# Small attention heads: each head's keys alone in a zero-padded 128-row tile, with a new state-space order and activation

## The chip, the cores and the metric

The kernel runs on one core of a Trainium2 chip. The metric is device microseconds of one launch. The time before is the median of three runs.

## The reference

Two layers of a hybrid network on an input of 4 x 512 tokens with 256 features, in float32. Each sublayer adds its output to x after a layer norm:

```python
x = x + state_space(ln(x))      # in-projection, conv of 4, silu, scan, gate, out-projection
x = x + ffn0(ln(x))
x = x + rotary_attention(ln(x)) # 16 heads of 16
x = x + ffn0(ln(x))
x = x + latent_and_pattern(ln(x))  # latent attention and 16 plain heads of 16, mixed by a gate
x = x + ffn1(ln(x))
x = x + grouped(ln(x))          # 32 query heads of 8 over 8 key heads, and a memory term
x = x + ffn1(ln(x))
```

The state-space recurrence is `h = exp(delta * A) * h + delta * B * u`, `y = C * h`, along 512 steps. Attention is `softmax(q @ k.T * scale) @ v` per head. The memory term of the grouped sublayer is

```python
sigma_q = jax.nn.elu(q.reshape(b, s, N_QUERY, D_KV))
a_mem = sigma_q @ memory / (sigma_q @ memory_norm)
out = a_dot * (1.0 - w) + a_mem * w      # w = sigmoid(memory_weight)
```

## The kernel before, in words

x stays in the core's memory, 128 features by 2 by 2048 tokens, and four batches of 512 tokens are worked on in turn. Nine stages follow each other (`PLAN`): state space, ffn0, rotary, ffn0, pattern, latent, ffn1, grouped, ffn1. A stage starts when the one before has ended on all engines (`stage_start`, line 183). Constants and weights come by SP's DMA queue; POOL cuts weights into a high and a low part (`cut_pieces`, line 209), and three matmuls of such parts (`mm3`, lines 226 to 228) stand for one product. The order on each engine is a list of events written out by hand; every engine walks the same list and does its share of each event, in that order, waiting on counters of the others.

**State space** (`mamba`, line 334; events at 364 to 394). In a batch: `wx` (in-projection on PE, copied by ACT), `conv` (four DVE operations, lines 592 and 596), `u` (silu on ACT, line 528), `u cut` (high part on ACT, line 534, low on POOL, line 438), `wz`, `steps` (a narrow product for delta, line 480), `one` and `delta` (softplus on ACT and DVE), then for each of four feature tiles `B` and `C` (12 matmuls each), `step` (spreads delta, line 500; ACT makes `a bar` from it, line 557) and `scan` (six DVE operations, lines 620 to 637, the first `du`, the last the gated product), `y cut` (line 564), and `out` in the next batch. The front of a batch (`mean`, `squared`, `var`, `dev`, `xn`, `xn cut`) is the layer norm; `dev` is a root on ACT (line 305).

**Small heads** (`Heads`, line 932) serve three stages: rotary and pattern with two heads to a 128-row tile (64 rows each, `per` = 2) and grouped with four (32 rows each). Four heads make a group g; there are 16 groups in rotary and in pattern and 32 in grouped. Selection matmuls (lines 1069 and 1070) stack queries (`eq`) and keys (`ek`) of a group from the high and low parts; ACT copies the stacks to `QS` and `KS` (lines 1101 and 1105), the keys with a row of ones. In rotary and pattern a group has two key tiles, in grouped the keys are stacked once a batch, two tiles. Then `mx`: 16 matmuls per group (line 1074), each followed by a maximum over keys on DVE (line 1137). `bias` (line 1079) turns the maxima, and DVE adds them to a row of the query stack (line 1143). `s` makes the scores, keys as weights (line 1084), ACT takes the exponential (line 1116), `pv` multiplies with the values, four heads side by side in 32 columns each (line 1091). Scores have three PSUM banks, other products four in turn.

A unit is a group and one of four key tiles `kt`. `schedule` (line 983) emits the four `s` of a unit with one to four `mx` of the next group between them, then the `pv` of the unit before, then what is in the slot: stacks two groups ahead after the last unit of a group, norms, projections of the next batch, and so on, set by `heads.put`.

```python
nc.tensor.matmul(self.psum(ev), self.QS[r, g % 2, h // self.per, q * P:(q + 1) * P],
                 self.k_of(g, self.k_tile_no(g, h))[r, :], start=True, stop=True)
```

Here `r` is the head's 64 or 32 rows, so a matmul uses those rows of the array alone.

**Grouped** (line 2155) adds the memory term: `qk`, then `tanh` (lines 2273 and 2278), `elu` (three DVE operations, lines 2330 to 2334, a reciprocal among them), `elu sum` on POOL (2300), `memory norm` and `memory` (fp32 products, line 2245), added to the attention by DVE (2351, 2354). For the first batch both halves of it stand in the start of the stage.

Of the kernel before, what the change touches and what calls it, by code (L numbers as in the profile page):

```python
# [18 lines left out]
F32 = mybir.dt.float32  # L19
F32R = mybir.dt.float32r  # L20
# [5 lines left out]
P = 128  # L26
# [123 lines left out]
def build(nc, io, out, plan, table):  # L150
    ctx = ExitStack()
    with ctx:
# [3 lines left out]
        def sem(name):  # L156
            return ctx.enter_context(nc.semaphore(name))
# [22 lines left out]
        x_in, c_in, stored = sem("x_in"), sem("c_in"), sem("stored")  # L180
# [153 lines left out]
        def mamba():  # L334
# [111 lines left out]
            def pe(pe, s):  # L446
# [7 lines left out]
                for ev in events:  # L454
# [6 lines left out]
                    if kind in ("mean", "var"):  # L461
                        if kind == "var":
                            pe.wait_ge(A.sem, A.at((s, ("squared", b))))
# [102 lines left out]
            def vec(dve, s):  # L566
# [13 lines left out]
                for ev in events:  # L580
                    kind, b = ev[:2]
                    if kind in ("mean", "var", "xn"):
                        if kind == "mean" and b:
                            dve.wait_ge(G.sem, G.at((s, ("xn cut", b - 1))))
# [347 lines left out]
        class Heads:  # L932
# [4 lines left out]
            def __init__(self, alloc, heads, width, rows, khead, scale, q_tile, k_tile, k_tiles, c, C, SEL):  # L937
# [10 lines left out]
                self.KS = alloc("k_stack", [P, 2, k_tiles or self.tiles, L], F32R)  # L948
# [27 lines left out]
            def k_of(self, g, t):  # L976

                return self.KS[:, (g // self.G4) % 2, t % self.k_tiles, :] if self.k_tiles else self.KS[:, g % 2, t, :]
# [1725 lines left out]
```

## Time and profile before

| | us |
|---|---|
| median of three runs | 4672.29 (4657.89 to 4677.12) |
| the profiled execution | 4669.16 |
| its span | 4667.3 |
| PE busy / DVE / ACT / POOL | 3906.4 / 2615.7 / 1657.6 / 1294.5 |
| state space, from start to 313 | 313 |
| ffn0, twice | 236 and 234 |
| rotary, 549 to 1063 | 514 |
| pattern, 1297 to 1746 | 449 |
| latent, 1746 to 2759 | 1013 |
| ffn1, twice | 560 and 560 |
| grouped, 3319 to 4101 | 782 |

The stages are read from the DMA that loads each stage's constants. PE is the busiest engine; matmuls overlap in the pipeline, and a busy share of PE is no share of its peak. The granted TensorE clock is given as a share of 2.4 GHz and is a mean over 0.5 and 1.0. Its mean over the span is 0.871.

### The profile page before, as it was taken

What the parts mean: (1) busy time and instruction counts of PE and PEld (TensorE: products, weight loads), DVE (VectorE), ACT (ScalarE), POOL (GpSimd) and SP (SyncE); (2) the same over time, 40 slices, a digit from 0 to 9 for tenths busy, and PEclk for the clock granted to TensorE, in tenths of its full rate; (3) what the DMA queues carried; (4) which work ended last, traced back from release to release, by engine and by line L of the source; (5) the groups of instructions that cost most, each with busy time, mean ns of one, the idle gap of its engine ahead of it and who ended that gap; (6) DMA issues with size and microseconds to landing.
All of it is one profiled execution on the core that took longest, in us unless ns stands there. A gap on an engine that the chain in (4) does not pass through costs nothing.

```text
span 4667.3 us, 44375 instructions
## 1 busy us (share of the span) xinstructions
PE 3906.4 (84%) x15840; PEld 2512.2 (54%) x15840; DVE 2615.7 (56%) x4363; ACT 1657.6 (36%) x2773; POOL 1294.5 (28%) x1034
## 2 busy tenths in 40 slices
PE   5769778887978874889889868999688888879999
PEld 4547544435844432556556647888433333347887
DVE  5545356654456643777777756333366666645333
ACT  2323246653235540333333323222244444422222
POOL 3224322214321003232323224443201110143442
PEclk8879889988979976999999989999866676679999
DMA  1010000001000001000000010000000000010000
GB/s 55 0 37 4 29 1 1 1 1 40 1 21 5 5 20 68 25 19 25 19 23 19 25 49 24 24 20 1 15 1 1 1 1 1 0 53 21 28 12 19
DMA packets 31815, 83.27 MB, mean 18 GB/s; under 512 B 6256, under 2 KB 7408, under 8 KB 31216
## 3 DMA queue, kind: packets, MB, share of 16 engines
q1 hardware_dynamic: 31600, 80.44, 5.5%
q8 instruction: 130, 2.13, 0.2%
q14 instruction: 85, 0.70, 0.1%
HBM read 59.44 MB, written 4.19 MB: 14 GB/s over the span
## 4 chain that ended last, share of the span: by engine, by line
PE 55%; DVE 21%; ACT 4%; POOL 2%; issue 2%; DMA 1%; SPq 1%; DVEq 0%; POOLq 0%; ACTq 0%
PE ps L226 10%; PE ps L227 10%; PE ps L228 10%; DVE max_cols L1137 6%; PE ps L1091 6%; PE ps L1084 3%; PE ps L1923 2%; PE ps L296 2%; DVE max_cols L2116 2%; DVE q_lo L2100 2%; PE ps L1074 2%; PE ps L1079 1%; ACT probs L1116 1%; PE ps L801 1%; PE ps L1069 1%
## 5 line engine op out<-in xcount | busy, mean ns | idle before, releaser
L1137 DVE TENSOR_REDUCE max_cols<-ps 128x1 fp32r<-128x512 f32 x1024 | 634.5, 680 | 274.2 <-PE ps L1074 249.1
L1116 ACT ACTIVATE probs<-ps 128x512 f32<-128x512 f32 x1024 | 538.3, 604 | 297.8 <-PE ps L1074 216.0
L755 POOL TENSOR_TENSOR h_lo<-h,h_hi 128x512 fp32r<-128x512 f32 x304 | 391.8, 1289 | 820.8 <-ACT h_hi L835 820.8
L912 DVE TENSOR_TENSOR gated<-silu,ps 128x512 f32<-128x512 f32 x288 | 198.0, 687 | 692.8 <-PE ps L228 664.5
L829 ACT ACTIVATE silu<-ps 128x512 f32<-128x512 f32 x304 | 181.7, 598 | 933.5 <-PE ps L228 933.3
L226 PE MATMUL ps<-xn_hi,w_hi 128*128 128x512 f32 x1216 | 481.5, 396 | 0.0
L227 PE MATMUL ps<-xn_lo,w_hi 128*128 128x512 f32 x1216 | 477.5, 393 | 0.0
L228 PE MATMUL ps<-xn_hi,w_lo 128*128 128x512 f32 x1216 | 477.0, 392 | 0.0
L1084 PE MATMUL ps<-q_stack,k_stack 64*128 64x512 f32 (+1 forms) x1024 | 415.6, 544 | 68.2 <-ACT probs L1116 63.9
L1074 PE MATMUL ps<-k_stack,q_stack 64*128 64x512 f32 (+1 forms) x1024 | 362.6, 532 | 80.1 <-DVE max_cols L1137 17.4
L1091 PE MATMUL ps<-probs,v_aug 128*32 128x512 f32 x2048 | 364.9, 794 | 0.0
L1084 PEld LDWEIGHTS ps<-q_stack,k_stack 64*128 64x128 f32 (+1 forms) x1024 | 171.2, 219 | 339.4 <-ACT probs L1116 175.7
L330 POOL CAST o_hi<-o_scaled 128x512 fp32r<-128x512 f32 x64 | 39.0, 610 | 1042.6 <-DVE o_scaled L1159 1042.6
L1923 PE MATMUL ps<-probs,v_tok 128*128 128x512 f32 x512 | 262.4, 609 | 2.7 <-ACT denominators L1985 2.7
L226 PEld LDWEIGHTS ps<-xn_hi,w_hi 128*128 128x128 f32 x1216 | 232.1, 191 | 50.0 <-issue 1.0
L227 PEld LDWEIGHTS ps<-xn_lo,w_hi 128*128 128x128 f32 x1216 | 231.5, 190 | 49.9 <-issue 1.5
L228 PEld LDWEIGHTS ps<-xn_hi,w_lo 128*128 128x128 f32 x1216 | 231.0, 190 | 48.9
L226 PE MATMUL ps<-h_hi,w_hi 128*128 128x512 f32 x608 | 250.2, 411 | 1.2 <-POOL h_lo L755 1.2
L1074 PEld LDWEIGHTS ps<-k_stack,q_stack 64*128 64x128 f32 (+1 forms) x1024 | 159.6, 216 | 165.7 <-ACT probs L1116 94.2
L227 PE MATMUL ps<-h_lo,w_hi 128*128 128x512 f32 x608 | 240.6, 396 | 0.0
L228 PE MATMUL ps<-h_hi,w_lo 128*128 128x512 f32 x608 | 240.4, 395 | 0.0
L1975 ACT ACTIVATE probs<-ps 128x1024 f32<-128x1024 f32 x128 | 131.1, 1024 | 279.3 <-PE ps L1920 279.2
(453 smaller groups left out, 7563.0 us busy)
## 6 DMA issues: line engine op xcount, KB each, us to landing
raw<-in_w_ffn SPq DMA_DIRECT2D x76, 448.0 KB, 3.3
raw<-raw SPq DMA_DIRECT2D x256, 64.0 KB, 2.0
composed_inputs<-in_m_latent SPq DMA_DIRECT2D x1, 5120.0 KB, 15.5
raw<-in_w_mamba SPq DMA_DIRECT2D x8, 448.0 KB, 6.1
raw<-in_w_latent SPq DMA_DIRECT2D x5, 448.0 KB, 16.8
x<-in_x SPq DMA_DIRECT2D x1, 2048.0 KB, 7.8
gated_pattern<-gated SPq DMA_DIRECT2D x4, 512.0 KB, 3.4
raw<-gated_pattern SPq DMA_DIRECT2D x4, 512.0 KB, 4.2
```

Of the source, the lines that this page charges most:

```text
L226: nc.tensor.matmul(psum, wh, xh, start=start, stop=False)
L227: nc.tensor.matmul(psum, wh, xl, start=False, stop=False)
L228: return nc.tensor.matmul(psum, wl, xh, start=False, stop=stop)
L755: nc.gpsimd.tensor_tensor(HL[:, b % 3, :], hb[:, b % 2, :], HH[:, b % 3, :].bitcast(F32), ALU.subtract).then_inc(G.sem, G.step((s, ev)))
L829: nc.scalar.activation(sg[:, i % 2, :], bank[i % 2], ACT.Silu).then_inc(A.sem, A.step((s, ev)))
L912: nc.vector.tensor_tensor(ga if routed(i) else hb[:, i % 2, :], sg[:, i % 2, :], bank[2 + i % 2], ALU.mult).then_inc(V.sem, V.step((s, "ga ...
L1074: last = nc.tensor.matmul(self.psum(ev), self.QS[r, g % 2, h // self.per, q * P:(q + 1) * P], self.k_of(g, self.k_tile_no(g, h))[r, :], st ...
L1084: last = nc.tensor.matmul(self.scores(self.step_no(g, kt, h)), self.k_of(g, self.k_tile_no(g, h))[r, kt * P:(kt + 1) * P], self.QS[r, g % ...
L1091: last = nc.tensor.matmul(bank[6][32 * h:32 * h + 32, :], self.VA[:, (g // self.G4) % 2, kt, self.khead((g % self.G4) * 4 + h), :], self.P ...
L1116: nc.scalar.activation(self.PB[:, n % 8, :], self.scores(n), ACT.Exp, scale=self.scale).then_inc(A.sem, A.step((s, ("exp", n))))
L1137: nc.vector.tensor_reduce(self.MB[:, self.tile_of(g, h) % 2, q, col:col + 1], self.psum(ev), op=ALU.max, axis=AX.X, negate=True).then_inc( ...
L1923: last = nc.tensor.matmul(bank[6 + i], VT[:, (g // HP) % 2, kt, 64 - 64 * i:192 - 64 * i], PB[:, (g * QT + kt) % 2, i, :], start=kt == 0, ...
```

## The change

Keys of each head stand alone in a 128-row tile whose other rows are zero (`KZ`, zeroed once by DVE at the start of a stage), so `mx` and `s` take all 128 rows of the query stack; the other heads' query rows meet zeros. ACT writes a key stack head by head: two operations in rotary and pattern, four in grouped, for one. In the state-space stage the event list is reordered and x is loaded in four DMAs. In grouped the elu becomes relu(q) + tanh(n/2) * (exp(n) + 1), with n = min(q, 0), its sums on POOL and no reciprocal; the first batch's memory term moves into the loop; the memory term is added to x by POOL.

```diff
             events = [(kind, 0) for kind in front] + [("wx", 0, m) for m in every] + [("conv", 0, m) for m in every]
-            events += [(kind, 1) for kind in front[:4]]
+            events += [(kind, 1) for kind in front[:4]] + [("u", 0, m) for m in every]
             for b in range(NB):
                 near, far = b + 1 < NB, b + 2 < NB
-                events += [("u", b, m) for m in every] + [("u cut", b, m) for m in every] + [("wz", b, m) for m in every]
+                events += [("u cut", b, m) for m in every] + [("wz", b, m) for m in every]
...
                 events += [("B", b, 0), ("one", b)]
-                events += [("wx", b + 1, 0), ("conv", b + 1, 0)] if near else []
+                events += [("wx", b + 1, 0)] if near else []
                 events += [("C", b, 0), ("delta", b)]
-                events += [("wx", b + 1, 1)] if near else []
-                events.append(("B", b, 1))
-                events += [("wx", b + 1, 2)] if near else []
-                events.append(("C", b, 1))
-                events += [("wx", b + 1, 3)] if near else []
-                events += [("step", b, 0), ("step", b, 1)]
-                events += [("conv", b + 1, 1)] if near else []
-                events += [("scan", b, 0), ("y cut", b, 0)]
+                events += [("wx", b + 1, 1), ("conv", b + 1, 0)] if near else []
+                events += [("step", b, 0), ("B", b, 1), ("step", b, 1), ("scan", b, 0), ("y cut", b, 0), ("C", b, 1)]
+                events += [("wx", b + 1, 2), ("conv", b + 1, 1), ("wx", b + 1, 3)] if near else []
+                events += [("scan", b, 1), ("y cut", b, 1)]
                 events += [("mean", b + 2), ("squared", b + 2)] if far else []
                 events += [("B", b, 2), ("step", b, 2), ("C", b, 2)]
-                events += [("conv", b + 1, 2)] if near else []
-                events += [("scan", b, 1), ("y cut", b, 1)]
-                events += [("var", b + 2)] if far else []
-                events += [("B", b, 3), ("step", b, 3), ("C", b, 3), ("scan", b, 2), ("y cut", b, 2)]
-                events += [("conv", b + 1, 3)] if near else []
+                events += [("conv", b + 1, 2), ("conv", b + 1, 3)] if near else []
+                events += [("scan", b, 2), ("y cut", b, 2)]
+                events += [("var", b + 2), ("dev", b + 2)] if far else []
+                events += [("B", b, 3), ("step", b, 3), ("C", b, 3)]
+                events += [("u", b + 1, m) for m in every] if near else []
                 events += [("scan", b, 3), ("y cut", b, 3)]
-                events += [("dev", b + 2)] if far else []
...
-                self.KS = alloc("k_stack", [P, 2, k_tiles or self.tiles, L], F32R)
+                self.alone = self.nkv if k_tiles else 4
+                self.KZ = alloc("k_alone", [P, 2, self.alone, L], F32R)
...
-                    r = slice((h % self.per) * self.rows, (h % self.per + 1) * self.rows)
-                    last = nc.tensor.matmul(self.psum(ev), self.QS[r, g % 2, h // self.per, q * P:(q + 1) * P],
-                                            self.k_of(g, self.k_tile_no(g, h))[r, :], start=True, stop=True)
+                    last = nc.tensor.matmul(self.psum(ev), self.q_rows(g, h)[:, q * P:(q + 1) * P], self.k_rows(g, h),
+                                            start=True, stop=True)
...
+                    if g == 0:
+                        act.wait_ge(V.sem, V.at((s, "alone")))
+                    for i in range(self.per):
+                        r = slice(i * self.rows, (i + 1) * self.rows)
+                        to = self.KZ[r, (g // self.G4 if self.k_tiles else g) % 2, t * self.per + i, :]
+                        nc.scalar.activation(to, self.psum(ev)[r, :], ACT.Identity, bias=self.one[r, :]).then_inc(A.sem, A.step((s, ev)))
...
+                nc.vector.memset(self.KZ[:, :, :, :].bitcast(F32), 0.0).then_inc(V.sem, V.step((s, "alone")))
...
+            a0, a1 = memory(0, 0), memory(0, 1)
+            heads.put(0, 0, 8, *a0[1])
+            heads.put(0, 1, 5, *a0[2])
+            heads.put(0, 0, 4, a1[0][0])
+            heads.put(0, 1, 8, a1[0][1])
+            heads.put(0, 2, 3, *a1[1])
+            heads.put(0, 2, 9, *a1[2])
+            begin = [(kind, 0) for kind in front] + [("qk", 0, 2)] + a0[0] + [("v", 0, q) for q in range(QT)]
...
-                        nc.scalar.activation(el, negative, ACT.Tanh, scale=0.5).then_inc(A.sem, A.step((s, ev)))
+                        act.wait_ge(G.sem, G.at((s, ("tanh",) + ev[1:])))
+                        nc.scalar.activation(half_tanh, negative, ACT.Tanh, scale=0.5).then_inc(A.sem, A.step())
+                        nc.scalar.activation(power, negative, ACT.Exp).then_inc(A.sem, A.step())
+                        nc.scalar.activation(whole, whole, ACT.Relu).then_inc(A.sem, A.step((s, ev)))
...
+                        nc.gpsimd.tensor_tensor(whole, CH[:, m, :].bitcast(F32), CL[:, m, :].bitcast(F32), ALU.add).then_inc(G.sem, G.step())
+                        pool.wait_ge(G.sem, G.last())
+                        nc.gpsimd.tensor_scalar(negative, whole, 0.0, None, ALU.min).then_inc(G.sem, G.step((s, ev)))
...
+                        nc.gpsimd.tensor_scalar(power, power, 1.0, None, ALU.add).then_inc(G.sem, G.step())
+                        pool.wait_ge(G.sem, G.last())
+                        nc.gpsimd.tensor_tensor(half_tanh, half_tanh, power, ALU.mult).then_inc(G.sem, G.step())
...
+                        nc.gpsimd.tensor_tensor(el, whole, half_tanh, ALU.add).then_inc(G.sem, G.step((s, ev)))
...
-                        nc.vector.tensor_scalar(t0, el, -1.0, 1.0, ALU.mult, ALU.add).then_inc(V.sem, V.step())
-                        after_last()
-                        nc.vector.reciprocal(t0, t0).then_inc(V.sem, V.step())
-                        after_last()
-                        nc.vector.scalar_tensor_tensor(t0, el, 2.0, t0, ALU.mult, ALU.mult).then_inc(V.sem, V.step((s, ev)))
...
-            sp.dma_start(x[:, :, :], io["x"]).then_inc(x_in, 16)
+            for b in range(NB):
+                sp.dma_start(x[:, :, b * L:(b + 1) * L], io["x"][:, :, b * L:(b + 1) * L]).then_inc(x_in[b], 16)
```

## Rows read from the trace of the kernel before

**Rows 1.** Windows: PE, PEld, DVE, ACT, POOL busy (count), clock, DMA share, GB/s.
```profile
640.00:1063.00 423.00, 359.26 (x1594) 173.80 (x1592) 266.13 (x444) 250.22 (x441) 87.86 (x80) 0.90 0.00 1
...
1352.00:1746.00 394.00, 328.93 (x1538) 164.14 (x1538) 233.94 (x392) 199.39 (x371) 40.35 (x38) 0.88 0.02 6
...
3395.00:4101.00 706.00, 597.80 (x2466) 234.11 (x2464) 459.55 (x749) 332.77 (x626) 77.93 (x76) 0.68 0.00 1
```
**Rows 2.** Windows of 20 us, in grouped and in rotary, same columns.
```profile
3480.00:3500.00 20.00, 17.83 (x76) 8.19 (x72) 11.23 (x20) 8.03 (x17) 0.43 (x1) 0.57 0.00 1
...
680.00:700.00 20.00, 18.43 (x83) 8.75 (x83) 12.94 (x22) 11.70 (x22) 1.90 (x2) 1.00 0.00 1
```
**Rows 3.** Timeline of PE: start, us, operation; two like units of grouped.
```profile
3495.80 1.94 PE L1091 MATMUL ps<-probs,v_aug 128*32 128x512 f32 x8
...
3501.29 1.08 PE L1091 MATMUL ps<-probs,v_aug 128*32 128x512 f32 x4
...
3676.37 1.06 PE L1091 MATMUL ps<-probs,v_aug 128*32 128x512 f32 x8
...
3679.76 0.64 PE L1091 MATMUL ps<-probs,v_aug 128*32 128x512 f32 x4
```
**Rows 4.** Timeline of PE: first of eight score and maximum matmuls, and what follows.
```profile
3418.64 0.79 PE L1084 MATMUL ps<-q_stack,k_stack 32*128 32x512 f32 x2
...
3421.26 1.94 PE L1091 MATMUL ps<-probs,v_aug 128*32 128x512 f32 x8
```
**Rows 5.** Timeline of PE at full clock, grouped.
```profile
3597.05 0.40 PE L2258 MATMUL ps<-o_lo,h_grouped_hi 128*128 128x512 f32 x1
3597.38 0.50 PE L1084 MATMUL ps<-q_stack,k_stack 32*128 32x512 f32 x1
3597.38 0.50 PE L1074 MATMUL ps<-k_stack,q_stack 32*128 32x512 f32 x3
...
3598.57 0.50 PE L1084 MATMUL ps<-q_stack,k_stack 32*128 32x512 f32 x1 [0.27 <-ACT probs L1116]
```
**Rows 6.** Timeline of the state-space stage, all engines, about its second batch.
```profile
119.38 0.63 ACT L564 ACTIVATE y_hi<-y 128x512 fp32r<-128x512 f32 x1 [8.15 <-DVE y L637]
...
122.95 2.19 ACT L528 ACTIVATE u<-u 128x512 f32<-128x512 f32 x4
...
127.75 0.63 PE L226 MATMUL ps<-u_hi,rate_hi 128*32 128x512 f32 x1 [9.88 <-ACT z L540]
...
142.96 2.33 DVE L596 SCALAR_TENSOR_TENSOR u<-padded,c,u 128x512 f32<-128x512 f32 x3
...
156.81 0.69 DVE L620 TENSOR_TENSOR du<-u,ps 128x512 f32<-128x512 f32 x1 [6.04 <-PE ps L296]
```
**Rows 7.** Timeline of pattern: stacks on ACT, then PE's fourth score matmul.
```profile
1447.85 0.69 ACT L1101 ACTIVATE k_stack<-ps,c 128x512 fp32r<-128x512 f32 x1 [2.33 <-PE ps L1070]
...
1448.43 0.59 ACT L1105 ACTIVATE q_stack<-ps 128x512 fp32r<-128x512 f32 x1
...
1450.62 0.49 PE L1084 MATMUL ps<-q_stack,k_stack 64*128 64x512 f32 x1 [0.51 <-ACT probs L1116]
```
**Rows 8.** Chain that ended last, in the start of grouped: start, us, what.
```profile
3347.39 0.43 PE ps L228
...
3353.66 3.36 DVE t L2332
...
3357.82 1.27 POOL elu L2300
...
3363.34 0.23 PE ps L227
...
3377.20 0.11 PE ps L2252
```
**Rows 9.** Timeline of the start of grouped, DVE.
```profile
3322.50 1.76 DVE L1127 MEMSET v_aug<- 128x2048 f32 x1 [0.38 <-issue]
...
3332.54 1.28 DVE L313 TENSOR_TENSOR xc<-x,ps 128x512 f32<-128x512 f32 x2 [7.63 <-PE ps L296]
```

More of the change, by code:

```diff
@@ L179, in build @@
         gated_pattern = nc.dram_tensor("gated_pattern", (P, KD, T), F32, kind="Internal").ap()
-        x_in, c_in, stored = sem("x_in"), sem("c_in"), sem("stored")
+        x_in, c_in, stored = [sem(f"x_in{b}") for b in range(NB)], sem("c_in"), sem("stored")
         raws, c_loads = [0], [0]
@@ L461, in pe @@
                     if kind in ("mean", "var"):
-                        if kind == "var":
+                        if kind == "mean":
+                            pe.wait_ge(x_in[b], 16)
+                        else:
                             pe.wait_ge(A.sem, A.at((s, ("squared", b))))
@@ L582, in vec @@
                     if kind in ("mean", "var", "xn"):
-                        if kind == "mean" and b:
-                            dve.wait_ge(G.sem, G.at((s, ("xn cut", b - 1))))
+                        if kind == "mean":
+                            dve.wait_ge(x_in[b], 16)
+                            if b:
+                                dve.wait_ge(G.sem, G.at((s, ("xn cut", b - 1))))
                         front_vec(dve, s, ev, psum(ev) if kind != "xn" else None, xc, sq, dev, roots)
@@ L974, in maxima, with k_rows, q_rows @@
                 return [("mx", g, t * self.per + i, q) for t in range(self.tiles) for q in range(QT) for i in range(self.per)]
-            def k_of(self, g, t):
-                return self.KS[:, (g // self.G4) % 2, t % self.k_tiles, :] if self.k_tiles else self.KS[:, g % 2, t, :]
+            def k_rows(self, g, h):
+                if self.k_tiles:
+                    return self.KZ[:, (g // self.G4) % 2, self.khead((g % self.G4) * 4 + h), :]
+                return self.KZ[:, g % 2, h, :]
+            def q_rows(self, g, h):
+                return self.QS[:, g % 2, h // self.per, :]
             def k_tile_no(self, g, h):
@@ L1082, in pe @@
                     g, kt, h = ev[1:]
-                    r = slice((h % self.per) * self.rows, (h % self.per + 1) * self.rows)
-                    last = nc.tensor.matmul(self.scores(self.step_no(g, kt, h)),
-                                            self.k_of(g, self.k_tile_no(g, h))[r, kt * P:(kt + 1) * P],
-                                            self.QS[r, g % 2, h // self.per, :], start=True, stop=True)
+                    last = nc.tensor.matmul(self.scores(self.step_no(g, kt, h)), self.k_rows(g, h)[:, kt * P:(kt + 1) * P],
+                                            self.q_rows(g, h), start=True, stop=True)
                 elif kind == "pv":
@@ L1100, in act @@
                     act.wait_ge(PE.sem, PE.at((s, ev)))
-                    nc.scalar.activation(self.k_of(g, t), self.psum(ev), ACT.Identity, bias=self.one).then_inc(A.sem, A.step((s, ev)))
+                    if g == 0:
[4 more added lines that the diff above has]
+                        nc.scalar.activation(to, self.psum(ev)[r, :], ACT.Identity, bias=self.one[r, :]).then_inc(A.sem, A.step((s, ev)))
                 elif kind == "eq":
@@ L2184, in memory @@
             def memory(b, m):
-                return [[("qk", b, m), ("tanh", b, m)], [("elu", b, m), ("elu sum", b, m)], [("memory norm", b, m), ("memory", b, m)]]
+                return [[("qk", b, m), ("tanh", b, m)], [("elu", b, m)],
+                        [("memory norm", b, m), ("memory", b, m), ("memory added", b, m)]]
             for b in range(1, NB):
@@ L2190, in grouped @@
                 heads.put(b - 1, 1, 2, ("qk", b, 2))
[L2191 removed]
+                for m, j in ((0, 3), (1, 6)):
                     a = memory(b, m)
@@ L2201, in grouped @@
                     heads.put(b + 1, 0, 8, ("out", b, 1))
-            begin = [(kind, 0) for kind in front] + [("qk", 0, 2)] + sum(memory(0, 0), []) + sum(memory(0, 1), [])
-            begin += [("v", 0, q) for q in range(QT)]
+            a0, a1 = memory(0, 0), memory(0, 1)
[6 more added lines that the diff above has]
+            begin = [(kind, 0) for kind in front] + [("qk", 0, 2)] + a0[0] + [("v", 0, q) for q in range(QT)]
             heads.schedule(begin, [("out", NB - 1, 1)],
```

48 lines of the change are left out of this document (21 added, 27 removed).

## Prediction

> **What bounds the kernel now.** I read the window view by stage first, because the change touches four of nine stages. In the three small-head stages, once their start is over, the granted TensorE clock is 0.90 (rotary, 423 us), 0.88 (pattern, 394 us) and only 0.68 (grouped, 706 us), with PE busy 83% to 85% of each [rows 1]. The reader is to see that the low clock does not come with an idle PE: in two 20 us windows PE is busy 17.83 and 18.43 us, yet the clock is 0.57 in the one and 1.00 in the other [rows 2]. The first is in grouped, whose score matmuls have 32 rows, the second in rotary, where they have 64. In the chain, a series of 128-row matmuls begins at 0.43 us apiece (1.2 GHz) and is at 0.23 later (2.4 GHz) [rows 8]. So I take rows of the array, not busy time, as what the clock follows here. What the clock is worth stands in the timeline of PE: the same unit of work (one `pv` to the next) takes 5.49 us at clock 0.5 and 3.39 us at 1.0, so 38% of the slow time is lost [rows 3]. PE sets the end in both: its neighbours wait for it. In the state-space stage the bound alternates between PE and DVE: after the last gated product of a batch PE waits for ACT and POOL (to 127.75), and then DVE waits for PE and ACT (to 156.81) [rows 6].
>
> The sum is made against the profiled execution's 4669.2 us (span 4667.3 and 1.9 around it). The median of the runs is 3.1 us above, which I add at the end.
>
> **State-space order.** Before `step 0` PE no longer issues `B 1`, `wx 2`, `C 1`, `wx 3`: 36 matmuls of 0.23 us [rows 8], 8.3 us in batches 0 to 2, and 24, or 5.5 us, in batch 3 (no next batch): -30.4. Two things come back. One more convolution (2.33 us for three of its four operations [rows 6], 2.9 in all) stands inside DVE's scan chain where it stood ahead of it: +8.7. And the root `dev` now stands on ACT ahead of the last `a bar`. DVE's last scan waits for that, with nothing else in its queue, over two table loads, the root and the exponential. The 2.94 us between the end of `y hi` and the first `u` (loads and root) [rows 6] plus 0.6 make 3.5 us, in two batches: +7. At the border of batches, root, loads (2.9) and the four `u` activations (2.19) no longer stand between `y hi` and the step matmuls: -5.1 twice, and -3.5 once where there is no root: -13.7. Part sum **-28** (bounds -44 with nothing given back, 0 if DVE's chain takes it all). Four x loads for one: SP issues three more DMAs ahead of the constants, while the first mean needs a quarter of x: 0, bounds +2 and -2.
>
> **Rotary and pattern.** Each key stack becomes two ACT operations. Back to back they start 0.58 us apart [rows 7], two more per group. Queued behind them are the query stacks and the exponentials; the fourth score matmul of the next unit waits for the first of these already (0.51 us [rows 7]), and the `pv` and maxima for it. Nothing covers it, so 28 groups x 1.16 = **+33** (bounds 0 if later waits absorb it, +36 with those at the start).
>
> The score and maximum matmuls no longer run side by side. Four now share one stretch of 0.50 us [rows 5], and eight at 1.2 GHz take 2.62 us [rows 4] where eight 128-row ones of 0.43 would take 3.44: 0.8 more, 0.4 at full clock. Five of the eight stand before the fourth score matmul, which waits 1.19 us from the first for the exponentials anyway [rows 5]; five times 0.23 is 1.15, covered. The three behind it pay: 0.15 x 128 units = +19. Against that, every second border between unlike shapes costs about 0.1 us less (the step from a 128-row matmul at 3597.05 to the first score matmul is 0.33 [rows 5], against 0.23 between like ones): -8. Together **+11**.
>
> A rule speaks against the change here. First the row: a burst of eight that takes 2.62 us today cannot lose more than the 0.82 that single file adds [rows 4, 8], so side-by-side running saves a quarter and no more. The Trainium skill, "TensorE: Matmul & The Clock Gate", section "Part 3: Packing small matmuls", says to slice small contractions into distinct row groups, and gives 3.07x for four 32-row matmuls. By that ratio each of the 256 units would lose 1.2 us and the sum would be +171 instead of -123. The row excludes it, so it gets no chance of its own.
>
> Clock: (1 - 0.90) x 2 x 423 and (1 - 0.88) x 2 x 394 make 180 us at half clock [rows 1]. I take 60% of it as gone and 30% of that time as gained (less than the 38%, since more units here wait for ACT): **-32** (bounds 0 and -54).
>
> **Grouped.** 0.64 x 706 = 452 us at half clock [rows 1]. Between the 38% [rows 3] and some 28% where the unit waits for maxima I take 34%. If the stage ends at a clock of 0.92 (a little above rotary's, now that all score matmuls fill the array), about 93 us stay slow, so 359 x 0.34 = **-122** (bounds 0 and -154). Side-by-side lost: 19 less 6 = **+13**. Keys: eight ACT operations for two, 6 x 0.58 x 4 batches = **+14**. Activation: the two serial passes of the start (reciprocal 3.36 us on DVE, POOL, two fp32 products each) run from 3353.66 to 3377.20, 23.5 us [rows 8]. They leave it; their matmuls, about 9 us, return inside the loop, and some 2.5 us of the new POOL and ACT chain stay uncovered: **-12**. In the loop ACT is held for two POOL operations (1.27 each at most by [rows 8]) and two more of its own, about 2.3 us longer, six times (+14), while DVE loses 4.5 us of in-order work each time in front of maxima and bias. Half on the path is -14: **0**, bounds +20 and -20. New memory additions run on POOL, idle there most of the time. The large memset of the key tile is at most 4 x 1.76 = 7.0 us on DVE in grouped; it is hidden by the 7.63 us for which DVE waits for PE [rows 9], and would cost what sticks out, under 2 us. Sum **-107**.
>
> Total: -28 + 33 + 11 - 32 - 107 = **-123**, so 4546, and 4549 us beside the median.
>
> **Rivals.**
> *A, slower: the clock does not follow rows.* Then the grants stay, and the unpacked matmuls are paid at 1.2 GHz. In grouped 0.64 of 128 units pay 0.8 and the rest 0.15: +73, less 6, plus 14, less 12 = +69. Rotary and pattern +44, state space -28: +85, **4757 us**. For it: PE is already busy 85% and the grant still falls, and zeros add no work. Against it: [rows 2] and the rise within one 128-row series. With f the share of grouped's slow time that turns fast, and the other stages in step, the sum is about 85 - 240 f; it decides at f = 0.35, a clock in grouped of about 0.79. The skill's page "TensorE: Matmul & The Clock Gate", "Part 1", describes the grant as set by how busy the PE has been; taken as busy time alone, that rule gives this rival. Chance 0.09.
> *B: DVE and ACT become the bound in grouped.* DVE is busy 460 us of 706 [rows 1], some 420 after the reciprocals leave; PE at full speed needs 128 x (8 x 0.23 + 1.06) = 371 for scores, maxima and `pv` [rows 3, 8] and, an estimate, 120 for the rest. With both near each other, each maximum and bias waits in turn, and half of the clock's gain stays off: +61, **4610 us**. For: `bias` and `s` wait in turns on DVE and ACT already. Against: the 3.39 us unit contains those waits. Chance 0.22.
> *C: everything at full clock and the key copies absorbed.* -32 more in grouped, -22 in the other two, and up to -47 of key copies: **4448 us**. Chance 0.14.
> The forecast has 0.55.
>
> **How the numbers follow.** The range 4470 to 4645 holds the forecast with the bounds of the state-space term and of the key copies, B, and half of C. About 0.1 lies above (A and a little of B) and 0.08 below. A measurement of this kernel can tell about 0.5%, 23 us, from no change. Faster: forecast, C and nearly all of B, 0.87. Within 0.5%: 0.04, from B with the state-space gain lost. Slower: A, 0.09.
>
> **What would show it.** Right: grouped's granted clock at 0.88 or more and its stage near 675 us (782 now); score and maximum matmuls 128 rows deep, starting 0.23 us apart and not together; rotary and pattern within 15 us of before, with a longer wait for ACT in front of the fourth score matmul after each stack; state space near 285 us (313 now), its first `du` of a batch about 8 us nearer to the step matmuls. Wrong: a clock in grouped under 0.79; or a full clock with grouped above 720 us, DVE then busy over 80%; or rotary and pattern longer by more than 20 us each, which would put the key copies above what I priced.

## The result, and the profile after

The changed kernel takes 4604.62 us (median of 4 runs, 4602.95 to 4616.60) against 4674.70 for the kernel before on the same chip: ratio 0.986, 95% interval 0.983 to 0.989. By medians the gain is 70 us of the 123 forecast. The profiled execution took 4616.6 us, 12 above its median, with a span of 4614.8, so the two profiled spans are 52.5 us apart (70 short of the forecast), and the stages below add up to that. The mean granted clock rose from 0.871 to 0.919. Further down, every ratio is to runs of the kernel before on the same chip; its median was 4662 to 4675 us on the chips used.

First the stages, read as before from the DMA of each stage's constants on SP's timeline of the changed kernel.

```profile
294.39 0.33 SPq L728 DMA_DIRECT2D c<-in_c_ffn  x1
...
529.84 0.33 SPq L272 DMA_DIRECT2D c<-in_c_rotary  x1
...
1064.88 0.33 SPq L728 DMA_DIRECT2D c<-in_c_ffn  x1
...
1300.57 0.33 SPq L272 DMA_DIRECT2D c<-in_c_pattern  x1
...
1762.32 0.33 SPq L1755 DMA_DIRECT2D c<-in_c_latent  x1
...
2781.86 0.33 SPq L728 DMA_DIRECT2D c<-in_c_ffn  x1
...
3341.18 0.33 SPq L272 DMA_DIRECT2D c<-in_c_grouped  x1
...
4048.98 0.33 SPq L728 DMA_DIRECT2D c<-in_c_ffn  x1
```

| stage | before | after | change | forecast |
|---|---|---|---|---|
| state space | 313.1 | 294.4 | -18.7 | -28 |
| rotary and pattern | 514.2 + 449.3 | 535.0 + 461.8 | +33.3 | +12 |
| grouped | 782.2 | 707.8 | -74.4 | -107 |
| the five others | 2601.6 | 2609.1 | +7.5 | 0 |

The other five run the same code in both kernels; their sum ends where the output's DMA is issued, and the 7 us behind that are in both. Over all kernels here ffn0 came out between 230.5 and 236 us and latent between 1012 and 1023, so a difference of some 6 us in one stage of one profile is not read as an effect. The 461.8 of pattern is such a case: five other profiles below with the same code in that stage (e2, e3, e4, e7, e8) have 456.2 to 457.2, e7 at a clock of 0.97 where this one has 0.94. Rotary and pattern together are 988.1 to 994.7 us in those five (963.5 before, 996.8 here).

The windows that answer [rows 1], same columns: rotary, pattern, the start of grouped (64 us, 76 before), its loop.

```profile
622.00:1065.00 443.00, 376.48 (x1590) 201.29 (x1588) 266.75 (x444) 274.64 (x469) 87.94 (x80) 0.92 0.00 1
1357.00:1762.00 405.00, 337.35 (x1538) 189.90 (x1537) 234.15 (x392) 224.74 (x401) 40.54 (x38) 0.94 0.02 6
3341.00:3405.00 64.00, 32.60 (x88) 19.14 (x89) 29.20 (x39) 17.99 (x30) 15.67 (x15) 0.71 0.08 27
3405.00:4049.00 644.00, 539.14 (x2466) 277.10 (x2464) 428.38 (x722) 354.60 (x649) 128.50 (x113) 0.93 0.00 1
```

In grouped the clock went from 0.68 to 0.93 at an unchanged busy share of PE (85%, now 84%). ACT's busy time grew in all three, by 24 us in rotary: these are the key copies (in grouped the new activation's operations are among them).

The matmuls, PE's timeline in grouped, answer to [rows 5]. They now stand 128 rows deep and start 0.22 to 0.23 us apart, where four of 32 rows shared one stretch.

```profile
3693.73 0.39 PE L1079 MATMUL ps<-k_alone,q_stack 128*128 128x512 f32 x1
3693.96 0.39 PE L1088 MATMUL ps<-q_stack,k_alone 128*128 128x512 f32 x1
3694.18 0.62 PE L1079 MATMUL ps<-k_alone,q_stack 128*128 128x512 f32 x2
3694.64 0.39 PE L1088 MATMUL ps<-q_stack,k_alone 128*128 128x512 f32 x1
```

The stacks in pattern answer to [rows 7]. From the first copy to the first exponential ACT works without a pause for 3.95 us. In the kernel before, four such operations take 2 x 0.57 + 2 x 0.48 = 2.10 us. The fourth score matmul waits 1.56 us for ACT (0.51 before).

```profile
1382.80 1.39 ACT L1109 ACTIVATE k_alone<-ps,c 64x512 fp32r<-64x512 f32 x2 [1.48 <-PE ps L1076]
...
1384.21 0.60 ACT L1113 ACTIVATE q_stack<-ps 128x512 fp32r<-128x512 f32 x1
1384.84 1.39 ACT L1109 ACTIVATE k_alone<-ps,c 64x512 fp32r<-64x512 f32 x2
...
1386.25 0.60 ACT L1113 ACTIVATE q_stack<-ps 128x512 fp32r<-128x512 f32 x1
1386.75 2.06 ACT L1124 ACTIVATE probs<-ps 128x512 f32<-128x512 f32 x4
...
1387.39 0.50 PE L1088 MATMUL ps<-q_stack,k_alone 128*128 128x512 f32 x1 [1.56 <-ACT probs L1124]
```

The activation inside grouped's loop, all engines. ACT holds its queue for two POOL operations (`whole`, `negative`), with the exponentials behind it, and PE stands for 3.95 us.

```profile
3695.10 1.27 POOL L2315 TENSOR_TENSOR whole<-heads_hi,heads_lo 128x512 f32<-128x512 f32 x1 [10.86 <-DVE heads_lo L2354]
...
3696.46 1.49 POOL L2317 TENSOR_SCALAR negative<-whole 128x512 f32<-128x512 f32 x1
3697.98 0.63 ACT L2289 ACTIVATE half_tanh<-negative 128x512 f32<-128x512 f32 x1 [3.69 <-POOL negative L2317]
...
3700.18 0.79 PE L1088 MATMUL ps<-q_stack,k_alone 128*128 128x512 f32 x1 [3.95 <-ACT probs L1124]
```

The state-space stage, DVE's timeline, answers to [rows 6]: the first, third and fourth `du` (the first operation of a scan) of one batch, then the first `du` of the next.

```profile
86.34 0.69 DVE L619 TENSOR_TENSOR du<-u,ps 128x512 f32<-128x512 f32 x1 [0.59 <-ACT a_bar L554]
...
107.62 0.68 DVE L619 TENSOR_TENSOR du<-u,ps 128x512 f32<-128x512 f32 x1
...
117.16 0.69 DVE L619 TENSOR_TENSOR du<-u,ps 128x512 f32<-128x512 f32 x1 [3.78 <-ACT a_bar L554]
...
147.63 0.69 DVE L619 TENSOR_TENSOR du<-u,ps 128x512 f32<-128x512 f32 x1 [3.28 <-ACT a_bar L554]
```

The first and the fourth of the same batch in the kernel before:

```profile
90.08 0.69 DVE L620 TENSOR_TENSOR du<-u,ps 128x512 f32<-128x512 f32 x1 [5.34 <-PE ps L296]
...
114.21 0.68 DVE L620 TENSOR_TENSOR du<-u,ps 128x512 f32<-128x512 f32 x1
```

First to fourth is 30.8 us where it was 24.1, fourth to the next first 30.5 where it was 42.6 (to 156.81 [rows 6]).

### The profile page after: what moved, and what is told of

It reads as the page before. It is cut to its first block, busy times and chain, and to the rows that moved or that the text cites. A ratio compares the mean times of both kernels' runs of the same rounds, so it can differ in the third digit from the quotient of the medians.

```text
span 4614.8 us, 44490 instructions
## 1 busy us (share of the span) xinstructions
PE 3872.1 (84%) x15840; PEld 2607.8 (57%) x15840; DVE 2593.4 (56%) x4326; ACT 1741.8 (38%) x2871; POOL 1351.3 (29%) x1074
## 4 chain that ended last, share of the span: by engine, by line
PE 53%; DVE 22%; ACT 6%; POOL 3%; issue 2%; DMA 1%; SPq 1%; DVEq 0%; POOLq 0%; ACTq 0%
PE ps L226 10%; PE ps L227 10%; PE ps L228 10%; DVE max_cols L1146 7%; PE ps L1094 4%; PE ps L1932 3%; PE ps L1079 2%; PE ps L296 2%; PE ps L1088 2%; ACT k_alone L1109 2%; DVE q_lo L2109 2%; DVE max_cols L2125 2%; PE ps L800 1%; ACT q_stack L1113 1%; PE ps L1084 1%
## 5 line engine op out<-in xcount | busy, mean ns | idle before, releaser
L1124 ACT ACTIVATE probs<-ps 128x512 f32<-128x512 f32 x1024 | 550.2, 602 | 240.2 <-PE ps L1088 231.4
L1088 PE MATMUL ps<-q_stack,k_alone 128*128 128x512 f32 x1024 | 430.3, 442 | 86.7 <-ACT probs L1124 83.0
L1079 PE MATMUL ps<-k_alone,q_stack 128*128 128x512 f32 x1024 | 405.7, 434 | 73.2 <-ACT q_stack L1113 33.6
L1088 PEld LDWEIGHTS ps<-q_stack,k_alone 128*128 128x128 f32 x1024 | 200.0, 197 | 234.6 <-ACT probs L1124 163.1
L1079 PEld LDWEIGHTS ps<-k_alone,q_stack 128*128 128x128 f32 x1024 | 202.9, 199 | 198.5 <-ACT probs L1124 59.6
L1094 PE MATMUL ps<-probs,v_aug 128*32 128x512 f32 x2048 | 299.4, 659 | 0.0
```

The costliest lines, as they stand in the source:

```text
L1079: last = nc.tensor.matmul(self.psum(ev), self.q_rows(g, h)[:, q * P:(q + 1) * P], self.k_rows(g, h), start=True, stop=True)
L1088: last = nc.tensor.matmul(self.scores(self.step_no(g, kt, h)), self.k_rows(g, h)[:, kt * P:(kt + 1) * P], self.q_rows(g, h), start=True, s ...
L1094: last = nc.tensor.matmul(bank[6][32 * h:32 * h + 32, :], self.VA[:, (g // self.G4) % 2, kt, self.khead((g % self.G4) * 4 + h), :], self.P ...
L1124: nc.scalar.activation(self.PB[:, n % 8, :], self.scores(n), ACT.Exp, scale=self.scale).then_inc(A.sem, A.step((s, ("exp", n))))
```

## The experiments

**e1: the row slices back.** The changed kernel; score and maximum matmuls read only their head's rows of the same tiles. This prices the full rows with all the rest held.

```diff
-self.q_rows(g, h)[:, q * P:(q + 1) * P], self.k_rows(g, h)
+self.q_rows(g, h)[r, q * P:(q + 1) * P], self.k_rows(g, h)[r, :]
```

> The changed kernel, but each score and maximum matmul takes its own 64 or 32 rows again, out of the same zero-padded key tiles and with the same split key copies. Theory (the granted clock follows the rows of the array that are used): grouped falls back to a clock near 0.68 and its stage grows from 708 us to 790 to 830; in all 4700 to 4750 us. Rival (clock follows busy time, and what made it rise was something else in the change): clock stays near 0.91 in grouped, the matmuls run side by side again, 4570 to 4600 us.

Measured 4712.7 us, ratio 1.010 (1.005 to 1.016): slower than before. Rotary 548.3, pattern 480.9, grouped 787.7, 2 us under the least expected for it. Grouped's loop:

```profile
3427.00:4150.00 723.00, 594.53 (x2469) 234.82 (x2468) 428.25 (x722) 349.46 (x649) 127.92 (x113) 0.69 0.00 1
```

The full rows are worth 13.3, 19.1 and 79.9 us in the three stages, 112 in all, and an edit of nothing but the depth of the operands moves grouped's clock from 0.69 to 0.93. PE's busy share is 82% at the one and 84% at the other. The edit changes two things together: the rows that a matmul uses, and whether four matmuls share a stretch or run one after the other. Which of the two the clock answers to, no run here separates; and a matmul at half clock lasts longer (0.43 us against 0.23 [rows 8]), so an equal busy share is not equal work. The Trainium skill's "TensorE: Matmul & The Clock Gate", "Part 1", says that the grant follows how busy PE has been. Taken as the share of time in which matmuls run, this pair of profiles disagrees.

**e2: keys alone, nothing else.** The kernel before with the changed `Heads`.

> The kernel before with the keys of each head alone in all three small-head stages and nothing else of the change. Theory: it carries most of the gain by itself; grouped at a clock of 0.9 or more, state space at 313 us again, so 19 us more than the changed kernel, and the old activation within 15 us of the new: 4605 to 4640 us. Rival (the new activation carries the gain in grouped): grouped stays above 750 us and the whole above 4650 us.

Measured 4630.7 us, ratio 0.993 (0.991 to 0.995). Rotary 534.0, pattern 456.2, grouped 718.3 at a clock of 0.94 in its loop, state space 314.5: as expected, and the two other parts make up the rest.

**e4: the old activation in the changed kernel.** The function `grouped` of before.

> The changed kernel with the grouped stage's old activation and old place of the first batch's memory term. Theory: ACT no longer waits for two POOL operations six times in the loop (3.3 us each, -20), the reciprocals are back on DVE (half of 27 us on the path), the start is 12 us longer: grouped 700 to 720 us against 708. Rival (the activation is the whole reason why grouped gained less than forecast): grouped under 690 us.

Measured 4616.1 us, ratio 0.990 (0.985 to 0.994), grouped 720.7, 0.7 over what was expected. The first `pv` of the stage comes 89.1 us after its start (67.5 with the new activation), and from the first to the last are 620.8 us (630.5). So the new activation takes 21.6 us from the start and puts 9.7 back in the loop.

**e5: key copies split, tiles shared.** The kernel before with each key copy written head by head into the same stack.

```diff
-nc.scalar.activation(self.k_of(g, t), self.psum(ev), ACT.Identity, bias=self.one)
+for i in range(self.per):
+    r = slice(i * self.rows, (i + 1) * self.rows)
+    nc.scalar.activation(self.k_of(g, t)[r, :], self.psum(ev)[r, :], ACT.Identity, bias=self.one[r, :])
```

> The kernel before, with each key stack copied by one ACT operation per head instead of one per tile, into the same shared tile; matmuls as before. Theory (price from the changed trace, 1.85 us a group): rotary and pattern +24 to +30 us each, grouped +12 to +18 us, in all 4730 to 4750 us. Rival 1 (price of the forecast, 1.16 us a group and 3.5 a batch): +47, about 4720 us. Rival 2 (copies are absorbed by later waits, and the longer rotary and pattern of the changed kernel come from single-file matmuls): within 15 us of before.

Measured 4771.6 us, ratio 1.023 (1.018 to 1.027), some 107 us longer: dearer than any of my prices. Rotary +37.1, pattern +28.2, grouped +37.3 against the profile of before, and the clock of the span fell from 0.871 to 0.855: from 0.90 to 0.85 in rotary's loop (459 us), 0.88 to 0.87 in pattern's (421 us) and 0.68 to 0.64 in grouped's (743 us), with no matmul touched. Set beside e2 (grouped 718.3 against 819.5), the full rows are worth 101 us there.

**e3: the old state-space order in the changed kernel.**

> The changed kernel with the state-space stage's old order of events (the per-batch loads of the input and all the rest of the change stay). Theory: the new order alone gives the stage's gain, so the stage goes from 294.4 us back to 313, and the kernel to about 4623 us (4612 to 4634). Rival: most of the 18.7 us comes from the input arriving in quarters, since the first batch can start before the whole of it is there; then the stage stays under 300 us and the kernel within 4600 to 4612.

Measured 4622.2 us, ratio 0.989 (0.986 to 0.992), state space 316.0, 3 us more than before: the order alone gives the stage's gain, and the quartered input none of it.

**e8: the root behind the last scan.** The changed kernel.

```diff
-events += [("var", b + 2), ("dev", b + 2)] if far else []
+events += [("var", b + 2)] if far else []
...
 events += [("scan", b, 3), ("y cut", b, 3)]
+events += [("dev", b + 2)] if far else []
```

> The changed kernel, but the deviation root of batch b+2 goes back behind the last scan of batch b, so that it no longer stands ahead of the fourth decay tile. Theory: VectorE's two waits of 3.78 us for that tile (at 117 and 178 us) go and the state-space stage falls by 7 us, 294.4 to 287 (kernel 4598, 4590 to 4604). Rival: the root is then late for the normalization that follows, and what is saved at the tile is given back there: stage 293 to 297.

Measured 4605.2 us, ratio 0.985 (0.981 to 0.989), state space 291.9. That is neither the theory's 287 nor in the rival's 293 to 297, but 1.7 of the 2.5 us under the changed kernel lie ahead of the first `du`, which this edit cannot reach; behind it the stage is 0.8 us shorter. The rival's mechanism held. DVE's timeline of e8:

```profile
84.69 0.69 DVE L620 TENSOR_TENSOR du<-u,ps 128x512 f32<-128x512 f32 x1 [0.59 <-ACT a_bar L555]
...
112.44 0.69 DVE L620 TENSOR_TENSOR du<-u,ps 128x512 f32<-128x512 f32 x1 [0.72 <-ACT a_bar L555]
...
119.91 0.25 DVE L320 RECIPROCAL few<-roots 128x16 f32<-128x16 f32 x1 [2.33 <-ACT roots L305]
...
145.90 0.69 DVE L620 TENSOR_TENSOR du<-u,ps 128x512 f32<-128x512 f32 x1 [3.28 <-ACT a_bar L555]
```

The wait for the decay tile falls from 3.78 to 0.72 us, and a wait of 2.33 for the root appears. First to fourth `du` is 27.8 us (30.8), fourth to the next first 33.5 (30.5): 3 us saved and 3 given back. The root's table loads cost the same at either place, to within that 0.8 us.

**e6: whole-tile copies.** The changed kernel; each copy writes all 128 rows, scaled by a 0/1 column of its head (two small columns made by DVE at the start), and the zeroing goes.

```diff
-nc.scalar.activation(to, self.psum(ev)[r, :], ACT.Identity, bias=self.one[r, :])
+nc.scalar.activation(to, self.psum(ev), ACT.Identity, scale=self.own[:, i:i + 1], bias=self.ones_at[:, i:i + 1])
```

> The changed kernel, but each key copy writes all 128 rows of its tile, scaled by a 0/1 column for its head, and the zeroing of the key tiles goes. In the changed kernel row-sliced copies start 0.707 us apart, in the kernel before a whole-tile copy with the same bias was followed after 0.570. Theory: the slice of rows is what costs, and the pitch falls to 0.57: 160 copies x 0.137 = 22 us of ScalarE time, most of it waited for by TensorE, so 4585 us (4575 to 4595), rotary and pattern some 8 us shorter each. Rival: the operand read per partition costs, and a second one (the scale) costs as much again: pitch 0.70 or more, time 4600 to 4620.

Measured 4585.9 us, ratio 0.981 (0.978 to 0.985); rotary 528.4, pattern 450.5, grouped 705.5. ACT's timeline in pattern:

```profile
1371.75 1.46 ACT L1109 ACTIVATE k_alone<-ps,ones_at,own 128x512 fp32r<-128x512 f32 x2
1373.07 0.62 ACT L1114 ACTIVATE q_stack<-ps 128x512 fp32r<-128x512 f32 x1
1373.55 2.10 ACT L1125 ACTIVATE probs<-ps 128x512 f32<-128x512 f32 x4
```

The time is the theory's, its reason only half right. Copies now start 0.663 us apart, not 0.57 (1371.75 to 1373.07 is two), and what follows the query copy starts 0.48 behind it instead of 0.62. The slice cost 0.14 us and is gone; the second per-row operand costs 0.09 again, the rival's point. The Trainium skill's "ScalarE: Activation LUTs", "What ACT_TABLE_LOAD costs", gives 93 ns for each such operand and as much overlap between operations. For whole tiles the trace agrees on the operand (0.477 us apart without one, 0.570 with one, 0.663 with two) and shows more overlap, 0.12 us (0.597 long and 0.477 apart). For the changed kernel's slices it shows none: each ran to its end first (0.682 long, 0.707 apart). The zeroing, a memset on DVE, went with the same edit; its share was not measured alone.

**e7: ACT's activation one slot group later.** The changed kernel; the POOL pair is an event of its own ("low") where "tanh" stood, and "tanh" goes from slot 2 to slot 5.

```diff
-return [[("qk", b, m), ("tanh", b, m)], [("elu", b, m)],
+return [[("qk", b, m), ("low", b, m)], [("elu", b, m)],
...
 heads.put(b - 1, j, 2, *a[0])
+heads.put(b - 1, j, 5, ("tanh", b, m))
```

> The changed kernel, but inside the grouped loop ScalarE's three activation steps are queued one slot group later than GpSimd's two steps that they wait for. Theory: what the new activation costs in the loop (9.7 us against the old one, with TensorE waiting 29.5 us for ScalarE's probabilities where the old one had it wait 2.5) is ScalarE standing for GpSimd; the grouped stage falls from 707.8 to about 698 us and the kernel to 4595 (4588 to 4602). Rival: the cost is the three activations' own 2.3 us six times, which the queue pays wherever they stand: stage 704 to 710, kernel unchanged.

Measured 4572.4 us, ratio 0.979 (0.976 to 0.982), grouped 683.0. The 24.8 us gained in the stage are well over the 10 expected, and the kernel's time is below the whole range given. The view of waits of both kernels, of grouped's loop, us in total, times and longest; first the changed kernel, then e7:

```profile
PE ps L1084 <- DVE max_cols L1146: 30.9, 28, 1.4
PE ps L1088 <- ACT probs L1124: 29.1, 11, 4.0
PE ps L1079 <- ACT q_stack L1113: 19.2, 23, 4.9
```

```profile
PE ps L1084 <- DVE max_cols L1146: 29.9, 28, 1.4
PE ps L1079 <- ACT q_stack L1113: 19.0, 22, 4.9
...
PE ps L1088 <- DVE o_scaled L1168: 6.9, 6, 1.2
PE ps L1088 <- ACT probs L1124: 5.6, 6, 3.4
```

PE's wait for the probabilities falls by 23.5 us, a wait of 6.9 us for DVE's `o_scaled` is new, and the other waits stay: 18 us less in all (99.2 to 81.0). The rest of the 24.8 us was not traced further; the clock of the loop is 0.95 where it was 0.93. In the changed kernel ACT waits for POOL's `negative` 4.74 us once and 3.69 six times, here 4.74 once and 0.90 six times.

**f1: keys alone in grouped only**, with whole copies as in e6 and the activation as in e7; rotary and pattern keep the shared stacks with single copies and 64-row operands.

> Keys alone in the grouped stage only; rotary and pattern keep two heads to a key tile, one copy and 64-row operands as before. In grouped the copies write whole tiles (as in e6) and ScalarE's activation stands one slot group later (as in e7); the new state-space order stays. Theory: in rotary and pattern the copies cost more than the clock gives back, so these stages return to 514 and 449 us, grouped stays at e7's 683 less e6's 2, and the kernel comes to 4542 us (4532 to 4552), below both kernels. Rival: much of what rotary and pattern lost lies elsewhere than in the key copies; then they stay above 520 and 455 and the kernel is at 4555 to 4575.

Measured 4540.5 us, ratio 0.972 (0.969 to 0.976). Rotary 511.3, pattern 450.0, grouped 678.4. In rotary and pattern the change as made was a loss, and undoing it there gets the whole of it back.

**f3: the key copies shared by two engines.** e7, with ACT copying the lower half of a tile's heads and DVE the upper half; PE waits for both.

```diff
-for i in range(self.per):
+for i in range(self.per // 2):
...
+for i in range(self.per // 2, self.per):
+    nc.vector.tensor_scalar(to, self.psum(ev)[r, :], self.one[r, :], None, ALU.add)
```

> e7 with the key copies shared: ScalarE copies the lower half of a tile's heads, VectorE the upper half, in slices of rows as in the changed kernel. Theory: the copies cost by ScalarE's queue alone (six instructions, 3.95 us, where 2.10 stood before); with a third of it gone to VectorE, 1.4 us nearer in each of 30 groups, up to 42 us of which I expect half: 4550 us (4535 to 4562), rotary and pattern some 8 us shorter each. Rival: VectorE's copy stands behind the row maxima (0.68 us each) that it is running, so the stacks come no sooner and the maxima come later: 4572 to 4595.

Measured **4486.9 us, ratio 0.961 (0.957 to 0.964)**, with nothing left out of the computation: the best version found, 118 us under the changed kernel. Against e7: rotary 500.2 (-34.7), pattern 425.3 (-31.3), grouped 661.5 (-21.4), 87 us where I had expected half of 42. ACT's timeline in pattern, and the window of grouped's loop:

```profile
1406.00 0.68 ACT L1112 ACTIVATE k_alone<-ps,c 64x512 fp32r<-64x512 f32 x1 [2.37 <-PE ps L1079]
1406.58 0.58 ACT L1116 ACTIVATE q_stack<-ps 128x512 fp32r<-128x512 f32 x1
1407.06 0.67 ACT L1112 ACTIVATE k_alone<-ps,c 64x512 fp32r<-64x512 f32 x1
1407.63 0.58 ACT L1116 ACTIVATE q_stack<-ps 128x512 fp32r<-128x512 f32 x1
1408.11 2.03 ACT L1127 ACTIVATE probs<-ps 128x512 f32<-128x512 f32 x4
```

```profile
3323.00:3920.00 597.00, 518.07 (x2454) 265.78 (x2453) 432.08 (x728) 341.23 (x632) 128.46 (x113) 0.97 0.00 1
```

First copy to first exponential is 2.11 us, what it was before the change. What remains on ACT in rotary and pattern are slices that begin at row 0, and these overlap with their neighbours again (0.57 and 0.48 apart), so a group saves 1.84 us where I had counted 1.4. That is 52 us in 28 groups of the 66 gained in the two stages; rotary's clock also rose, from 0.92 in e7 to 0.96. The rival, DVE's copies queued behind its maxima, cost less than ACT gave back: a copy of 64 rows takes DVE 0.756 us.

**f4 and g1: half maxima**, in the changed kernel and in the kernel before. Each row maximum is taken over 256 of 512 columns.

```diff
-self.psum(ev), op=ALU.max
+self.psum(ev)[:, 0:L // 2], op=ALU.max
```

> The changed kernel with every row maximum taken over 256 of the 512 columns (half of the keys are left out of the maximum; everything else is computed). The case in which VectorE is the bound of the grouped loop at full clock: its 492 maxima there go from 0.68 us to some 0.35, 160 us less of busy time, and the stage falls by over 60 us, below 648. Theory: VectorE is 67% busy there and TensorE waits 35.9 us for it in 54 short waits; these shrink and half of it comes back: grouped 707.8 to about 688 (680 to 698), kernel about 4570 (4555 to 4590).

> The kernel before with every row maximum over 256 of the 512 columns, half of the keys left out as in f4, where the maxima went from 0.680 to 0.418 us and the grouped stage lost 59.7 us, rotary 41.6, pattern 35. Theory (the bound moved): before the change TensorE's half clock covered VectorE in the grouped loop, so the same cut gives there less than 30 us (782.2 to 752 or more), and the part of the 59.7 us above that is a bound which only the faster clock laid bare; the kernel comes to about 4565 us (4545 to 4590), as rotary and pattern were mostly at full clock. Rival: the maxima bounded each burst in both kernels alike; then grouped loses 50 to 65 us and the kernel comes to 4515 to 4545.

f4 measured 4470.2 us, ratio 0.957 (0.954 to 0.961); rotary 493.4, pattern 426.6, grouped 648.1 (-59.7). g1 measured 4437.8 us, ratio 0.953 (0.949 to 0.957); rotary 463.8, pattern 386.1, grouped 648.8 (-133.4). The profiled execution of g1 is the fastest of its four, 20 us below their median, so its stages flatter it. The group of DVE's maxima in f4 (mean 418 ns; 680 in the changed kernel), then grouped's loop in f4 and in g1:

```profile
L1146 DVE TENSOR_REDUCE max_cols<-ps 128x1 fp32r<-128x256 f32 x1024 | 388.0, 418 | 392.0 <-PE ps L1079 384.6
```

```profile
3316.00:3900.00 584.00, 515.94 (x2444) 273.31 (x2442) 307.85 (x714) 348.90 (x643) 128.64 (x113) 0.94 0.00 1
```

```profile
3277.00:3850.00 573.00, 489.26 (x2456) 193.34 (x2454) 330.41 (x745) 326.54 (x621) 78.03 (x76) 0.83 0.00 1
```

My numbers fell in both runs, and the rival's in g1 too; f4 came out at the edge of what was expected if DVE is the bound. An engine that is 67% busy sets 60 us of a 708 us stage. The likely way, argued and not tried: the maxima come up to three to a slot, PE makes one in 0.23 us and DVE reads one in 0.68, and the bias matmul stands behind the last. PE's waits of over 0.15 us fall by 34 us in f4 (99.2 to 65.5), those for the maxima from 30.9 to 3.5; the other 26 us of the stage stay open. This was no bound that the faster clock laid bare: the kernel before loses more by the same cut, and its 32-row matmuls are then granted 0.83 where they had 0.68. DVE's maxima held that clock down too. The half-clock time of its loop falls from 452 us to 2 x 0.17 x 573 = 195; at the forecast's 34% that is, an estimate, 87 of the 133 us.

Set side by side, the two runs say when the change pays. With half maxima grouped takes 648 us with either layout, at a clock of 0.94 or 0.83, and rotary and pattern take 920.0 us with the changed kernel's copies and 849.9 with the shared stacks. f4 has the new activation besides, and g1's profile is 20 us under its median, so the comparison is rough; but the 80 to 101 us of the full rows in grouped were measured beside maxima of 0.68 us, and little is left of them beside 0.42. Shared copies with half maxima were not tried.

## Why the prediction came out as it did

The result lies in the range, and the likeliest case held in its mechanism: the clock rose with the full rows. Against the profiled execution 70 of the 123 us are missing (53 by medians), and a range of 175 us was wide enough for that. Of the signs that were to show it right, the clock and the depth and pitch of the matmuls came; grouped near 675 us did not (708), nor rotary within 15 us (+21; pattern +12.5), nor state space near 285 (294). Stage by stage the miss is 9 in state space, 21 in rotary and pattern, 33 in grouped and 7 in stages that nobody touched.

**Key copies: the term that was mis-sized.** The prediction took two more operations per group at 0.58 us, 1.16, "+33" for rotary and pattern and "+14" for grouped. e5 measured 65 and 37, e1 against before 66 for the first two, and f3 gave 66 back when half of the copies left ACT. My 0.58 was the pitch (start to start) of a whole-tile copy [rows 7]; four slices start 0.707 apart and the query copies lose their overlap as well, so a group pays 1.85 us, 52 in 28 groups. The rest goes with the clock, which e5 lowered in all three stages. An estimate: its time at half clock grew by 53, 15 and 83 us in the three loops, at the forecast's 30% and 34% some 20 us in rotary and pattern and 28 in grouped. On these figures the copies account for +33 and +23 of the 70 us. The 23 holds at 32-row operands; at 128 rows, where the clock is high, the price of grouped's copies was not measured alone, and f3 shows only that half of them leaving ACT gives 21 us there. The upper bound "+36" was too low, since it was made with the same pitch. In grouped all eight copies stand ahead of the query stack, for which PE waits up to 4.9 us.

**Clock: right.** The forecast said 0.88 or more; it is 0.93 in grouped's loop. Rows worth -122 + 13 = -109 in grouped measured -101 (e5 to e2) and -80 (e1 to after, where ACT's wait for POOL may hide a part; not tried); -32 + 11 = -21 in the other two measured -32 (e1 to after). Rival A asked for grants that stay as they were; in e1's pair they do not, whichever of its two differences the clock answers to. But "I take rows of the array, not busy time, as what the clock follows here" was too narrow: g1 raised the clock at 32 rows without touching an operand of a matmul, and e5 lowered it.

**Single file: seen, its price not.** Score and maximum matmuls stand 0.23 us apart, and e1, which pays nothing for single file, is slower in all three stages. The +11 and +13 for it were never measured apart from the clock.

**Activation: right in sum, and better than I saw.** -12 in grouped was the forecast, -12.9 the measurement (e4): 21.6 out of the start against "23.5 less 2.5", 9.7 back in the loop against "about 9". That ACT "is held for two POOL operations" was priced as covered; e7 shows that moving ACT out of this wait is worth 24.8 us.

**Memset: right.** It ran 6.88 us from 3348.27, and the first centred tile began at 3355.71, under 1 us after its matmul.

**State space: the direction right, two sizes off.** The way into the scans (first `du` from 90.1 to 86.3) and the three borders gave 3.7 + 12.1 + 12.9 + 9.1 = 37.8 us where the forecast had 30.4 + 13.7 = 44.1. The scan chains took back 6.7 + 6.7 + 3.8 + 2.4 = 19.6, not 15.7. The root ahead of the decay tile was placed and priced well (3.78 against 3.5), but e8 shows that it is not a cost of its place.

**Rival B** had 4610 us, near the result, and is not what happened, or only in part. B took DVE and ACT for a new bound that keeps half of the clock's gain off in grouped. In e7 the gain is there (683 us against "near 675"), at a DVE busy 69%. DVE's bursts of maxima do bind (f4), but they did so before as well (g1), and the forecast's unit times contained them. Of B's wait for ACT there is more: e7 shows 24.8 us of it, for a reason that B did not name. A number that is met does not prove its case: here it came from another term, in other stages too.

## What to carry to other kernels

Price an added operation by the same form in the trace; where that form does not occur, as a slice of rows here, let the bound include the full duration without overlap. Where a small copy stands between a product and an in-order queue of exponentials, give half of it to the engine beside it before deciding whether the layout pays: the same zero-padded layout lost 25 to 33 us in rotary and pattern with all copies on ACT and gained 38 with them shared (963.5 us before, 988.1 to 996.8, 925.5). To find a bound, halve the suspect's work and read the stage; the busy share would have cleared DVE. Run the same cut on the kernel before as well: here that showed how much of the layout's gain hangs on slow maxima.

## What the runs showed of the hardware

- Granted clock: at equal code 0.69 with 32-row operands and 0.93 with 128 rows, PE busy 82% and 84% (e1, after). At 32 rows it also rose from 0.68 to 0.83 when DVE's maxima went from 0.680 to 0.418 us (g1), PE busy 85% in both, and it fell to 0.64 when ACT's key copies were split (e5). Whether it answers to the rows or to the matmuls running side by side is open.
- ACT's operations on whole tiles start before the one ahead has ended (0.477 us apart at 0.597 long). With slices that begin at other rows between them they did not (0.707 at 0.682, and 0.623 from a query copy to the next key copy); where each copy on ACT is a slice that begins at row 0 they do (0.571, 0.477; f3, rotary and pattern). Why was not tried.
- A second per-row operand costs an ACT operation 0.09 us, like the first.
- POOL's TENSOR_SCALAR over 128x512 takes 1.49 us where its TENSOR_TENSOR takes 1.27.
